# A vision-transformer layer with top-2 experts: the drain of the attention loop, the weight casts and the placing of tokens rewritten

## What is computed

```
h = patches(x) @ W                                    # 2304 x 192
h = h + attention(layernorm(h)) @ W_o.T + b_o          # 12 heads of 16, causal, within an image
flat = layernorm(h)
probs = softmax(flat @ router_w.T)                     # 8 experts
top_w, top_i = top_k(probs, 2); top_w /= top_w.sum()
for e in range(8):
    w_e = sum(top_w * (top_i == e))
    out += w_e * (gelu(flat @ w1[e] + b1[e]) @ w2[e] + b2[e])   # 192 -> 768 -> 192
h = h + out
```

## Time and profile before

| what | value |
|---|---|
| median of three runs | 411.71 us |
| the profiled execution's own time | 414.29 us |
| its span, first to last instruction | 412.5 us |
| granted TensorE clock, mean of the span | 0.979 |
| TensorE (products) busy | 370.5 us, 90% |
| VectorE, ScalarE, GpSimd busy | 253.5, 217.1, 180.3 us |

### The profile page before, as it was taken

How to read it: one execution, slowest core, us unless ns; L and a number is a source line. 1 busy time by engine, 2 the same in 40 slices (tenths; PEclk the granted TensorE clock), 3 DMA queues, 4 the chain that set the end, 5 groups by cost and what they waited for, 6 DMA issues and landing times.

```text
span 412.5 us, 14891 instructions
## 1 busy us (share of the span) xinstructions
PE 370.5 (90%) x5740; PEld 327.1 (79%) x5740; DVE 253.5 (61%) x656; ACT 217.1 (53%) x443; POOL 180.3 (44%) x219
## 2 busy tenths in 40 slices
PE   3989999989999999997998889999999999999900
PEld 3879989979989899874454589999999999999800
DVE  4696468877877778785298154555445555445425
ACT  5668667778787786853233144444444444444300
POOL 8116322246455452317308545555555555553300
PEclk9999999999999999999999999999999999999965
DMA  8974004433344333361151213121223222121167
GB/s 255 311 252 150 15 21 127 134 87 102 97 119 116 81 86 92 109 186 32 51 130 50 59 31 89 55 86 57 80 61 88 80 60 84 55 58 42 38 254 274
DMA packets 29705, 42.82 MB, mean 104 GB/s; under 512 B 12416, under 2 KB 19440, under 8 KB 29640
## 3 DMA queue, kind: packets, MB, share of 16 engines
q1 hardware_dynamic: 25512, 33.37, 26.9%
q0 software_dynamic: 4128, 8.50, 7.4%
HBM read 30.23 MB, written 9.67 MB: 97 GB/s over the span
## 4 chain that ended last, share of the span: by engine, by line
PE 41%; issue 6%; DVE 5%; POOL 3%; DMA 3%; ACT 1%; SPq 0%; POOLq 0%; DVEq 0%
PE PSA L1259 19%; PE PSA L1274 15%; PE PSA L1137 3%; DMA W2h<-yrows 3%; POOL XF L477 2%; PE PSA L1278 2%; PE PSA L1226 2%; DVE PTR L938 1%; DVE H L1000 1%; POOL REG L484 1%; DMA yrows<-KBR 1%; DVE VB L935 1%; POOL REG L483 1%; PE PSA L1204 0%; SPq L444 0%
## 5 line engine op out<-in xcount | busy, mean ns | idle before, releaser
L1259 PE MATMUL PSA<-YT,W1h 128*128 128x128 f16 x774 | 78.0, 219 | 2.4 <-DVE YT L962 2.4
L1259 PE MATMUL PSA<-YT,W1l 128*128 128x128 f16 (+1 forms) x516 | 75.3, 220 | 0.0
L1274 PE MATMUL PSA<-W2h,PTR 128*128 x516 | 71.0, 246 | 0.3 <-DVE PTR L699 0.3
L516 POOL DMA_INDIRECT yrows<-KBR x43 | 43.0, 999 | 63.5 <-DVE KBR L977 63.2
L1259 PEld LDWEIGHTS PSA<-YT,W1h 128*128 x774 | 63.7, 98 | 6.6 <-DVE YT L962 2.8
L685 ACT ACTIVATE PTR<-PSA 128x768 f32<-128x768 f32 x43 | 34.8, 810 | 57.6 <-PE PSA L1259 52.7
L1274 PE MATMUL PSA<-W2l,PTR 128*128 x258 | 63.5, 246 | 0.0
L699 DVE SCALAR_TENSOR_TENSOR PTR<-PTR 128x768 f16<-128x768 f32 x43 | 41.2, 958 | 26.6 <-issue 14.2
L690 ACT ACTIVATE PTR<-PTR 128x768 f16<-128x768 f32 x43 | 36.3, 843 | 40.3 <-PE PSA L1278 40.1
L511 POOL DMA_INDIRECT REG<-xrows,KBR x43 | 42.6, 992 | 19.3 <-issue 11.6
L977 DVE TENSOR_SCALAR KBR<-PSA,KBR 128x192 f32<-128x192 f32 x43 | 18.0, 418 | 52.2 <-PE PSA L1278 52.2
(11 more groups left out here) (165 smaller groups left out, 805.6 us busy)
## 6 DMA issues: line engine op xcount, KB each, us to landing
WSTG<-w SPq DMA_DIRECT2D x16, 384.0 KB, 3.6
WSTG<-w SPq DMA_DIRECT2D x16, 336.0 KB, 3.2
REG<-xt SPq DMA_DIRECT2D x12, 324.0 KB, 5.4
W1l<-xt SPq DMA_DIRECT2D x10, 324.0 KB, 6.8
VB<-VP SPq DMA_DIRECT2D x99, 19.1 KB
H<-hrows SPq DMA_DIRECT2D x6, 288.0 KB
xrows<-REG SPq DMA_DIRECT2D x2, 800.2 KB
hrows<-H SPq DMA_DIRECT2D x1, 1296.0 KB
```

The lines of the kernel that those rows point to most:

```text
L516: gp.indirect_dma_start(out=yrows, out_offset=bass.IndirectOffsetOnAxis(ap=TARGET[:, s:s + 1], axis=0), in_=YO[s % 2], in_offset=None).the ...
L1259: ins = nc.tensor.matmul(bank(2 * u + f // (FC // 2), 128, FC // 2 * ST_)[:, w:w + ST_], weights[a, c], YT[0:rows, at:at + ST_], start=k = ...
L1274: nc.tensor.matmul(bank(4 + u, ST_, C), GP[a][:, at:at + ST_], weights[b], start=(f, a, b) == (0, 0, 0), stop=False)
```

## The change

**The drain.** The loop runs to step NT-2 = 20 on all four engines, and the rest is written out by hand. The last six tiles are handled in pairs (16,17), (18,19), (20,21). A pair has one cast, one pair of subtractions, six transposes into a bank of its own and one copy out. The rows of the first pair are normalised on GpSimd, those of the other two on VectorE (`late_rows`), and the subtraction of the last pair is on VectorE too (`last_low`). The products of tile 20 go to another bank, so that tile 21 does not wait for its residual; the logits of the last seven tiles go to bank 3.

**The weights.** `pieces(i)` gives every piece one step earlier: now two pieces in an even step, one in an odd one.

**The placing.** The parts are 14, 14 and 16 columns. VectorE multiplies the codes of a part, then compares the low parts of 14 columns by one instruction per column; ScalarE makes the last sixteen; GpSimd does nothing.

```diff
-        APART = VP[:, 0:TOPK * NT * ST_ // 4]
+        APART = VB[0:TT, TOPK * NT * HSTEP:TOPK * NT * HSTEP + 16 * ST_]
         def pieces(i):
-            return range(max(0, 3 * i // 2), min(2 * PIECES, 3 * (i + 1) // 2))
-        FIRST_NORM, GROUP, DRAIN = 8, 4, 3
+            return range(max(0, 3 * (i + 1) // 2), max(0, min(2 * PIECES, 3 * (i + 2) // 2)))
+        FIRST_NORM, GROUP = 8, 4
+        PAIRED = NT - 6
+        PAIRS = [(t, t + 1) for t in range(PAIRED, NT, 2)]
         def norm2_at(i):
-            at = {t: t + 5 for t in range(NT)}
-            at.update({t: NT - 1 + (t - (NT - 6)) // 2 for t in range(NT - 6, NT)})
-            return [t for t in range(NT) if at[t] == i]
+            return [i - 5] if 5 <= i < PAIRED + 5 else []
-        PARTS = [(a, a + TOPK * NT // 4) for a in range(0, TOPK * NT, TOPK * NT // 4)]
+        PARTS = [(0, 14), (14, 28), (28, TOPK * NT)]
...
@@ SyncE
-                sp.wait_ge(n2_row, b)
+                sp.wait_ge(h2_done, b)
...
@@ GpSimd
+            for t in PAIRS[0]:
+                norm2_row(t)
+            pair_low(PAIRS[0][0])
+            pair_low(PAIRS[1][0])
...
-            for n, (a, b) in enumerate(PARTS):
-                gp.wait_ge(high_placed, n // 2 + 1)
-                if n == 0:
-                    gp.wait_ge(ones_set, 5)
-                nc.gpsimd.tensor_tensor(at_high(a, b), at_high(a, b), CODE[:, a:b].unsqueeze(2).to_broadcast([TT, b - a, NS]),
-                                        ALU.mult).then_inc(coded, 1)
...
@@ ScalarE
-            for i in range(NT + DRAIN):
+            for i in range(NT - 1):
                 step(i)
+            exps(NT - 1)
+            norm2_out(PAIRED - 1)
+            probs_hi(NT - 1)
+            y_hi(NT - 2)
+            inverse_deviation(group(NT - 3))
+            y_hi(NT - 1)
+            pair_hi(PAIRS[0][0])
+            inverse_deviation(group(NT - 1))
+            pair_hi(PAIRS[1][0])
+            pair_out(PAIRS[0][0])
+            pair_hi(PAIRS[2][0])
+            pair_out(PAIRS[1][0])
+            pair_out(PAIRS[2][0])
...
@@ VectorE
+            def late_rows(t):
+                dve.wait_ge(rs_done, group(t) + 1)
...
+                for n in range(2):
+                    x = pair_source(t)[:, n * C:(n + 1) * C]
+                    nc.vector.tensor_scalar(x, htile(t + n), MEAN[:, NT + t + n:NT + t + n + 1], RS[:, NT + t + n:NT + t + n + 1],
+                                            ALU.subtract, ALU.mult).then_inc(late_row, 1)
...
-            for i in range(NT + DRAIN):
+            for i in range(NT - 1):
                 step(i)
+            for n in pieces(NT - 2):
+                piece_lo(n)
+            shift(NT - 1)
+            residual(NT - 3)
+            outputs(NT - 2)
+            stats2(NT - 3)
+            probs_lo(NT - 1)
+            logits(PAIRED - 1)
+            y_lo(NT - 2)
+            variances(group(NT - 3))
+            outputs(NT - 1)
+            refine(group(NT - 3))
+            y_lo(NT - 1)
+            residual(NT - 2)
+            stats2(NT - 2)
+            residual(NT - 1)
+            stats2(NT - 1)
+            variances(group(NT - 1))
+            late_rows(PAIRS[1][0])
+            refine(group(NT - 1))
+            late_rows(PAIRS[2][0])
+            last_low(PAIRS[2][0])
+            for t, _ in PAIRS:
+                pair_logits(t)
...
-            for n in (0, 2):
-                a, b = PARTS[n][0], PARTS[n + 1][1]
+            for a, b in ((0, NT), (NT, TOPK * NT)):
...
-            for a, b in PARTS[:-1]:
-                nc.vector.tensor_tensor(at_low(a, b), IOTA.unsqueeze(1).to_broadcast([TT, b - a, ST_]),
-                                        LOW[:, a:b].unsqueeze(2).to_broadcast([TT, b - a, ST_]), ALU.is_equal).then_inc(low_placed, 1)
+            for p, (a, b) in enumerate(PARTS):
+                dve.wait_ge(high_placed, p // 2 + 1)
+                if p == 1:
+                    dve.wait_ge(high_placed, 2)
+                nc.vector.tensor_tensor(at_high(a, b), at_high(a, b), CODE[:, a:b].unsqueeze(2).to_broadcast([TT, b - a, NS]),
+                                        ALU.mult).then_inc(coded, 1)
+                if p < 2:
+                    for n in range(a, b):
+                        nc.vector.tensor_scalar(AT_LOW[:, n * ST_:(n + 1) * ST_], IOTA, LOW[:, n:n + 1], None, ALU.is_equal).then_inc(low_placed, 1)
...
@@ TensorE
+            scores(NT - 1)
+            project(NT - 3)
+            outputs(NT - 2)
+            norm2_transpose(NT - 1, PAIRED - 1)
+            unread(1)
+            transpose_probs(NT - 1)
+            transpose_y(NT - 2)
+            router(NT - 1, PAIRED - 1)
+            unread(3)
+            outputs(NT - 1)
+            project(NT - 2)
+            unread(2)
+            transpose_y(NT - 1)
+            unread(3)
+            project(NT - 1)
+            unread(11)
+            pair_transpose(PAIRS[0][0])
+            unread(4)
+            pair_router(PAIRS[0][0])
+            pair_transpose(PAIRS[1][0])
+            unread(1)
+            pair_transpose(PAIRS[2][0])
+            pair_router(PAIRS[1][0])
+            unread(1)
+            pair_router(PAIRS[2][0])
...
-                unread(6 if p < 3 else 2)
-                if p < 3:
-                    pe.wait_ge(low_placed, p + 1)
+                unread(4)
+                if p < 2:
+                    pe.wait_ge(low_placed, b)
```

More of the change, by code:

```diff
@@ L405, in _ @@
             sp.wait_ge(consts_set, FILLS)
-            for i in range(-2, NT + 1):
+            for i in range(-2, NT):
                 for n in pieces(i - 1):
@@ L1115, in project @@
                 need(pe, yf_done, t + 1)
-                need(pe, lg_done, norm2_upto(t + 1))
+                need(pe, lg_done, min(norm2_upto(t + 1), PAIRED - 1))
                 n = 0
@@ L1127, in router @@
                 need(pe, lg_done, t)
-                need(pe, h2_done, upto(i - 1))
-                need(pe, yf_done, upto(i))
+                if t < PAIRED - 1:
+                    need(pe, h2_done, upto(i - 1))
+                    need(pe, yf_done, upto(i))
+                else:
+                    pe.wait_ge(sub_done, NT)
                 for k, (a, c, n) in enumerate(ROUTER_PRODUCTS):
-                    ins = nc.tensor.matmul(bank(6, TT, 512)[:, ROUT:ROUT + E], two(XT, t, 3 * TT)[:, n * TT:(n + 1) * TT],
+                    ins = nc.tensor.matmul(bank(router_bank(t), TT, 512)[:, ROUT:ROUT + E], two(XT, t, 3 * TT)[:, n * TT:(n + 1) * TT],
                                            WR[a][:, c * E:(c + 1) * E], start=k == 0, stop=k == len(ROUTER_PRODUCTS) - 1)
@@ L1139, in step @@
             def step(i):
-                late = i > NT - DRAIN
+                late = i == NT - 2
                 if late:
@@ L1143, in step @@
                     need(pe, vl_done, NT)
-                if has(i):
-                    scores(i)
-                if late and not has(i):
-                    unread(4)
+                scores(i)
                 if has(i - 2):
@@ L1159, in step @@
                     qk(i + 2, (0, 1))
-                if has(i):
-                    if late:
-                        unread(3)
-                    transpose_probs(i)
+                if late:
+                    unread(3)
+                transpose_probs(i)
                 if has(i + 2):
@@ L1173, in step, with early @@
                     transpose_y(i - 1)
+            def early(i):
+                if has(i + 3):
+                    v(i + 3)
+                if has(i + 2):
+                    qk(i + 2, (0, 1))
+                    qk(i + 2, (2, 3))
+                if has(i + 4):
+                    norm1_transpose(i + 4)
             for t in range(NT):
@@ L1181, in _ @@
                 if t in EMBEDDED:
-                    step(EMBEDDED[t])
-            for i in range(NT + DRAIN):
+                    early(EMBEDDED[t])
+            for i in range(NT - 1):
                 step(i)
+            scores(NT - 1)
[9 more added lines that the diff above has]
+            project(NT - 2)
+            unread(2)
+            transpose_y(NT - 1)
+            unread(3)
+            project(NT - 1)
[9 more added lines that the diff above has]
+            pair_router(PAIRS[2][0])
             unread(22)
@@ L1215, in _ @@
                     ins = placed(n, 5, n == 0, n == TOPK * NT - 1)
-                if b <= NT:
-                    for n in range(a, b):
-                        placed(n, 4, n == 0, n == NT - 1)
+                for n in range(a, min(b, NT)):
+                    placed(n, 4, n == 0, n == NT - 1)
             ins.then_inc(table_mm, 1)
```

81 lines of the change are left out of this document (73 added, 8 removed).

## The result

The changed kernel took 409.29 us (median of 8 runs, 406.55 to 414.08) beside 411.89 us of the kernel before on the same chip (8 runs, 411.39 to 412.30). The ratio is 0.9939 with a 95% interval of 0.9916 to 0.9962: faster, by 2.6 us and not by 6.5. (A run over 1.5% above the fastest of its kernel, as 414.08 here and 413.25 in e1, counts as slow and is left out of the ratio.) The runs spread over 7.5 us where those of before spread over 0.9, and they go with their mean granted clock: the fastest had 0.974, the slowest 0.951. That they go with the clock is the first hint. The spread alone is a weak one: in the later series the kernel before spread over 4.1, 3.0 and 3.0 us itself. The profiled run took 408.58 us, with a span of 406.8.

A forecast was written before the change was run, and what follows sets the result against it. The expert stage keeps TensorE full, so the kernel hangs on when its first tile is ready, behind drain, routing and placing. Drain -7.4, loop +1.3, placing -0.4 sum to -6.5: 411.7 to 405.2 us, range 402.8 to 408.2.

The forecast's parts named there:

- Part 1: Loop, weights one step earlier: refinement later in four group steps, about 0.33 us each, 1.3 us lost (bounds 0 to 2.8).
- That sign: Loop: TensorE's wait before norm2_transpose above 1 us in steps 6, 10, 14 and 18.
- Part 2: Drain, from scores of tile 21 to routing: 7.4 us gained, bounds 7.9 and 6.2.
- Step (c): Drain, from transpose_y of tile 21 to the end of the last refinement: 5.36 us, same work as before.
- Step (d): Drain, last pair from the last refinement to the routing: 4.9 us where it took 7.0.
- if TensorE waits between pairs: Drain: a sign that would show the prediction wrong; no size given.
- rival 3: Short drain: VectorE and GpSimd block each other (1.2 us), second group-step wait stays (1.1 more); 407.5 us, chance 0.09.
- Part 3: Placing, to the end of the table products: 0.4 us gained, with 0.16 us a comparison.
- rivals 1 and 2: Placing's comparisons: 1, fast, 403.2 to 404.3 us, chance 0.14; 2, slow, loss of 2.4, 408.0 us, chance 0.11.
- or if the granted clock falls in the drain: Drain: last of the signs that would show the prediction wrong; no size or chance given.

The follow-up runs named there:

- e1: Changed kernel with two weight pieces in odd steps and one in even ones, still one step early; 408.81 us, ratio 0.9860 to the kernel before.
- e4: Changed kernel with more fill products (unread) in drain and placing, weight schedule as in the change; 407.67 us, ratio 0.9867.
- e5: Changed kernel with two weight pieces in odd steps and more fill products in both drain and placing; 403.56 us, ratio 0.9804.
- e9: Changed kernel with two weight pieces in odd steps and more fill products in the drain alone; 407.43 us, ratio 0.9867.
- e12: e5 with GpSimd's subtractions of the first pair moved behind VectorE's moments of the last tile; 407.12 us, ratio 0.9853.
- e3: Changed kernel with the placing of the kernel before (GpSimd multiplies the codes, old fill); 411.33 us, ratio 0.9951.
- e8: e5 with nine more fill products before the third expert tile; 405.10 us, ratio 0.9871.
- e10: Changed kernel with two weight pieces in odd steps and more fill products in the placing alone; 409.45 us, ratio 0.9899.
- e6: Kernel before with 23 in place of 28 fill products ahead of the placing; 411.88 us, ratio 1.0014.
- e2: Kernel before with the change's weight schedule alone; 415.88 us, ratio 1.0059.
- e11: Changed kernel again, no edit, on the third series' chip; 411.12 us, ratio 0.9945.

## Why the prediction was right and wrong

**Part 1, forecast +1.3.** Right in size, partly wrong in place. Steps 6, 10 and 18 of the changed kernel took 7.97, 7.64 and 7.27 us, 0.23, 0.30 and 0.27 more than before (the same 0.27 in step 14 where the clock held): 1.07 in all. The prediction put the delay at `norm2_transpose` and expected over 1 us there; it stands at `project`, which the prediction had named as late next and judged no later. That sign was wrong, the price not. The scores of tile 21 came at 180.90 (forecast 180.4), the 0.78 of a clock fall in step 14 among it.

**Part 2, forecast -7.4.** The steps held one by one, from the scores on: `outputs` after 5.90 us (forecast 5.8), `transpose_y` after 7.78 (7.7), the last refinement after 13.55 (13.1), the routing after 18.78 (18.0). Step (c) took 5.77 us for 5.36; the two small VectorE instructions that waited out GpSimd's subtractions are 0.56 of it. Step (d) took 5.23 for 4.9: 0.2 more from the rows to the transposes, and 0.1 for each of the two routers. That makes -6.6, inside the bounds of -7.9 to -6.2. More fill does not shorten it: e4, with the change's weights and the drain filled, has 18.79 at a clock of 1.00. The 18.54 of e5 and e9 come from the weights, for with two pieces in the odd steps no low half stands ahead of `shift(21)` any more. The sign "if TensorE waits between pairs" came, with 0.72 and 0.65 us before two routers. Of rival 3, the short drain, a quarter came: half its block (0.56 for 1.2) and not its second wait.

**Part 3, forecast -0.4.** A comparison costs 0.162 us (forecast 0.16), so rivals 1 and 2 are out, and the last codes come 8.92 us after the first high comparison in e9 (forecast 8.8). But a table product costs 0.04 to 0.045 us and not 0.03, behind the four fill products that the prediction had counted: at full clock the change's placing takes 10.72 us (e9), against 10.69 before. So -0.4 was 0.0 up to the table, and with the fill of e5, where none stands before the last part, it is -0.83. What the prediction did not count is the way from there to the first expert product, 6.32 us in e9 for 6.71; with it part 3 comes to -0.36.

For the comparisons there was the rule of the Trainium skill, VectorE: DVE Perf Modes, The TRN2 errata, an estimated 0.094 us. The runs show 0.162, and the measurement decides. The same section says itself that this row comes out too low for single instructions, which the prediction passed over. The Trainium skill, SBUF — State Buffer, Who interferes with whom, says that a VectorE and a GpSimd instruction that both need the ports they share exclude each other for the whole instruction. The prediction saw only a partial hold-up in the placing; the four long instructions in the drains of e5 and e12 agree with the rule.

**The step that failed** is the sum's silent term: every duration was taken at the granted clock of 1.00 that the kernel before has throughout. The text had it as a last sign ("or if the granted clock falls in the drain") and gave it neither a price nor a chance. At full clock the three parts measure +1.07 - 6.63 - 0.36 = -5.9 (e3 and e4 for the loop, e4 for the drain, e9 for the placing), which makes 406.0 of 411.89. The median was 409.29, 3.3 more. The falls in the profiled run cost 0.78 in step 14, 1.02 in the routing and 12.09 - 10.72 = 1.37 in the placing: 3.2 together. That the two agree so well is partly luck, as the falls move from run to run, and the rest is taken as unchanged. Without the clock the sum was 0.6 us off, -5.9 for -6.5, and steps (c) and (d) of the drain are most of that. What moves less is in the table. With the new drain as the change fills it, the routing took 11.4 to 12.3 us in five profiles of five, over four kernels; with the filled drain 10.3 in six of six, over six kernels (e8 and e12 among them). In e9 against e10 on one chip, the drain's fill was worth 2.0 us more than the placing's. So that the clock costs this time, and that the fill takes the drain's fall away, is shown.

The old drain had waits too: TensorE idled 2.59 of its 25.42 us, with single waits of 1.17, 0.71 and 0.42, and kept its clock. The new one idles 2.46 of 18.78. The edits of e4 and e5 put fill in four places, each a wait of 0.5 to 1.8 us: `project` of tile 21, two routers, and the first table product. They leave 0.82 us of idle time in the drain of e4, and 0.45 in that of e9. Why the new drain loses the clock where the old one kept it isn't shown; that it does so where these waits stand, and not where they are filled, is. More than half of the 5.9 us was handed back by TensorE, which was not on the path of the drain until its own fill products, at half speed, came to stand before the rank products.

**What stays open.** Which wait makes the clock fall. Single waits of 0.45, 0.65 and 0.90 us were followed by a fall in one execution and by none in another; one of 1.8 us, with only 0.4 us of idle time in the ten before it, by none in e6. Three profiles of three show the placing's fall where the drain's had come before, and e9 shows none without it, but e9's own slower runs forbid to call that shown. The wait before the third expert tile, which every kernel has, shows the same: where it was 1.84 to 2.05 us, the clock fell behind it in five profiles (e2, e3, e4, e10, e12) and not in four (before, e1, e9, e11); at 1.05 us and less never, in five. For e12 that fall (231.5 to 235 us) is part of what it lacks against e5. The traces show where the second microsecond of that wait comes from. ScalarE, idle since the placing, starts its first instruction of the expert stage 1.91 us behind the first expert product in those five executions, and 2.70 to 2.91 us behind it in the other nine; the copy that TensorE then waits for follows 2.6 us later in all of them. Here is that instruction in e5, whose first expert product starts at 224.29, and in e12, where it starts at 224.43:

```profile
226.20 0.81 ACT L730 ACTIVATE PTR<-PSA 128x768 f32<-128x768 f32 x1 [11.41 <-PE PSA L1415]
```

```profile
227.33 0.81 ACT L731 ACTIVATE PTR<-PSA 128x768 f32<-128x768 f32 x1 [12.41 <-PE PSA L1416]
```

What makes ScalarE late isn't known; kernels of either placing and either weight schedule are on both sides. It is not known either where e9's clock fell in its slower runs, or what cost e8 its place: none of those executions was profiled.

## What to carry to other kernels

When an edit takes idle or filled time out of a stretch in front of TensorE, price its waits twice: once as time, and once as the chance that the products behind them run at half clock. Look for fill or other products that stand in TensorE's queue before the next thing that is waited for. If the mean granted clock of a kernel's runs is below that of the kernel before, and the slower runs have the lower clock, fill the waits first, and put no fill before the last product that the next stage needs. In this kernel that, and moving the second weight piece off the steps with a refinement, brought 7.7 us (ratio 0.9804, five runs in one series) where the change brought 2.6 (0.9939). On the other chip the nearest kernel, e12, had 0.9853, so the full gain still wants a repeat.

## Hardware that was not expected

- A wait of 0.45 to 2 us can be followed by some 3 to 8 us at or near 1.2 GHz (138 to 142, 200 to 203, 216 to 223 in the changed kernel, 55 to 63 in e10), and for identical code it comes or not: behind the same wait of 0.90 us a step took 8.36 us in e10 and 5.55 in e5.
- A VectorE instruction on 108x2 numbers in SBUF, 0.16 us alone, took 0.38, 0.53, 0.62 and 0.43 when it started inside a GpSimd subtraction, and ended with it to within 0.02 us.
- A comparison of 128 f16 elements with a per-partition operand costs VectorE 0.162 us in a row of fourteen.
- ScalarE's first instruction after 11 to 15 us of idleness started 1.91 us behind the first expert product in five executions and 2.70 to 2.91 us behind it in nine. In five of these nine TensorE's clock fell behind the longer wait that followed, in none of the five others.
